# A fused decoder layer on one core: attention values multiplied for two pairs of heads at a time, with a new order of the small steps around them

## What is computed

```python
x = x + attn(layernorm(x))        # h = rmsnorm(.); q, k, v = h @ wq, wk, wv (16 heads of 64)
                                  # softmax(q k^T / 8) v, then w_out, b_out
x = x + xattn(k=v=ctx, q=layernorm(x))   # one head of 128 over 512 rows, then Wo, bo
x = x + ffn(layernorm(x))         # quant_linear -> relu -> quant_linear
# quant_linear: x to 0..255 by the maximum of the WHOLE x, w to int8 by the row's maximum
```

## Time and profile before

| | us |
|---|---|
| median of 3 runs (402.93 to 403.12) | 403.11 |
| the profiled execution | 403.67 |
| its span on the core | 401.7 |
| TensorE busy | 379.6 (94%) |
| VectorE busy | 325.9 (81%) |
| ScalarE busy | 259.6 (65%) |
| GpSimd busy | 164.0 (41%) |

### The profile page before, as it was taken

How to read it: one execution, slowest core, us unless ns; L and a number is a source line. 1 busy time by engine, 2 the same in 40 slices (tenths; PEclk the granted TensorE clock), 3 DMA queues, 4 the chain that set the end, 5 groups by cost and what they waited for, 6 DMA issues and landing times.

```text
span 401.7 us, 9053 instructions
## 1 busy us (share of the span) xinstructions
PE 379.6 (94%) x2983; PEld 286.1 (71%) x2983; DVE 325.9 (81%) x777; ACT 259.6 (65%) x807; POOL 164.0 (41%) x179
## 2 busy tenths in 40 slices
PE   8899999999999999999999999999999999988675
PEld 7678777787777777777778777777777767656222
DVE  4869778869897789869895989778986998557895
ACT  4967676756768556767675666756676776515574
POOL 3645534534544345434454444434542444401000
PEclk9989999999999999999999999999999999999699
DMA  7500000001000100001000100010000000000003
GB/s 234 147 15 2 2 2 0 2 3 39 2 3 0 41 0 0 0 0 39 0 0 0 39 0 0 0 39 0 0 0 0 28 1 2 0 2 0 0 2 104
DMA packets 12310, 7.50 MB, mean 19 GB/s; under 512 B 1280, under 2 KB 11264, under 8 KB 12288
## 3 DMA queue, kind: packets, MB, share of 16 engines
q1 hardware_dynamic: 11856, 6.69, 5.6%
q10 hardware_dynamic: 432, 0.52, 0.5%
HBM read 6.16 MB, written 1.05 MB: 18 GB/s over the span
## 4 chain that ended last, share of the span: by engine, by line
PE 64%; DVE 20%; issue 10%; ACT 4%; DVEq 1%; POOL 1%; POOLq 0%; ACTq 0%
PE turned_bank L460 13%; PE o_bank L469 12%; PE score L450 11%; PE acc_bank L476 5%; DVE pT L911 4%; DVE negmax L904 4%; PE side_bank L433 3%; PE q_bank L433 3%; PE side_bank L527 3%; PE q_bank L435 3%; PE q_bank L434 3%; DVE h_max L1220 2%; PE side_bank L434 2%; PE side_bank L435 2%; PE side_bank L523 2%
## 5 line engine op out<-in xcount | busy, mean ns | idle before, releaser
L1264 POOL TENSOR_TENSOR prob<-prob,rinv 128x512 f32<-128x512 f32 x128 | 132.6, 1043 | 149.5 <-DVE rinv L908 149.4
L725 ACT ACTIVATE prob<-score,negmax 128x256 f32<-128x256 f32 x252 | 117.3, 473 | 71.8 <-DVE negmax L904 70.1
L904 DVE TENSOR_REDUCE negmax<-score 128x2 f32<-128x512 f32 x126 | 85.8, 682 | 28.1 <-PE score L450 26.8
L911 DVE COPY pT<-turned_bank 128x512 f32<-128x512 f32 x128 | 86.9, 679 | 11.5 <-PE turned_bank L460 11.1
L460 PE MATMUL turned_bank<-ident,prob 128*128 128x128 f32 x512 | 84.1, 287 | 3.9 <-DVE pT L911 3.4
L460 PEld LDWEIGHTS turned_bank<-ident,prob 128*128 128x128 f32 x512 | 53.9, 141 | 37.4 <-issue 26.0
L469 PE MATMUL o_bank<-pT,v_sb 128*64 128x256 f32 x512 | 69.4, 392 | 0.8 <-DVE pT L911 0.8
L725 ACT ACTIVATION_READ_ACCUMULATOR prob<-score,negmax 128x1 f32 x252 | 50.9, 202 | 0.0
L716 ACT ACTIVATE q_hi<-q_bank 128x512 fp32r<-128x512 f32 x63 | 38.0, 603 | 11.9 <-PE q_bank L435 11.0
L469 PEld LDWEIGHTS o_bank<-pT,v_sb 128*64 128x64 f32 x512 | 31.0, 136 | 19.9 <-issue 7.2
L896 DVE TENSOR_TENSOR q_lo<-q_bank,q_hi 128x512 fp32r<-128x512 f32 x63 | 42.7, 680 | 0.0
(11 more groups left out here) (229 smaller groups left out, 614.8 us busy)
## 6 DMA issues: line engine op xcount, KB each, us to landing
c_sb<-in_ctx_dram SPq DMA_DIRECT2D x8, 256.0 KB, 3.0
x_sb<-in_x_dram SPq DMA_DIRECT2D x8, 128.0 KB, 2.7
out_dram<-xn_all SPq DMA_DIRECT2D x4, 256.0 KB, 2.3
big<-in_L_attn_wk_dram ACTq DMA_DIRECT2D x2, 256.0 KB, 4.7
big<-in_L_attn_wq_dram SPq DMA_DIRECT2D x2, 256.0 KB, 5.7
big<-in_L_attn_wv_dram SPq DMA_DIRECT2D x2, 256.0 KB, 6.4
wo_sb<-in_L_attn_w_out_dram SPq DMA_DIRECT2D x1, 512.0 KB, 7.7
w_sb<-in_L_ffn_w_dram SPq DMA_DIRECT2D x2, 256.0 KB, 4.7
```

The lines of the kernel that those rows point to most:

```text
L725: last = nc.scalar.activation(prob[:, slot, t, :], banks[r][:, t * S:(t + 1) * S], ACT.Exp, bias=negmax[:, slot, t:t + 1], scale=1.0, accu ...
L904: nc.vector.tensor_reduce(negmax[:, slot], banks[r][:].rearrange("p (t k) -> p t k", k=S), X_AXIS, ALU.max, negate=True).then_inc(max_done, 1)
L911: nc.vector.tensor_copy(pT[:, slot].rearrange("p k q -> p (k q)"), turned_bank[:]).then_inc(pT_done, 1)
L1264: nc.gpsimd.tensor_tensor(prob[:, slot], prob[:, slot], rinv[:, slot].unsqueeze(2).to_broadcast([P, QT, S]), ALU.mult).then_inc(prob_done, 1)
```

## The change

In even steps TensorE now multiplies the values of two pairs, into both halves of `o_bank`, and ScalarE copies both with one instruction; in odd steps TensorE takes the output projections of two pairs. `pT` has 8 places in place of 4 for this. ScalarE does an even step's second side task after both exponentials, where it stood between them. VectorE does `split_lo` ahead of the maxima, where it stood behind them; in step 1 the `residual` stands behind the maxima, and `aggregate(1)` and GpSimd's `inverse_root(1)` move from step 1 to step 2. At the start `weights_lo(0, 1, 4)` comes before the third inversion. In the last batch the last three steps turn through three banks, `TL` moves from (7,0) to (7,1), rounding the feed-forward weights moves from step 3 to behind the steps, and the last two values use a bank each. In the feed-forward block two `keep_warm` are added, and both products of the second half have a bank for each chunk.

```diff
-LAST_PLACE[7, 0] = "TL"
+LAST_PLACE[7, 1] = "TL"
-        pT = sb("pT", [P, 4, QT, S])
+        pT = sb("pT", [P, 8, QT, S])
-        yT_banks = [q_banks[0], o_bank]
-        y_banks = [side_bank, score_bank[0]]
+        yT_banks = [q_banks[0], o_bank, *pT_bank]
+        y_banks = [side_bank, *score_bank, acc_bank]
+        def turned_in(kind, j, r):
+            if late(kind, j):          # kind == "last" and j >= PAIRS - 3
+                return (turned_bank, *q_banks)[(2 * (j - PAIRS + 3) + r) % 3]
+            return turned_bank
+        def copied_before(kind, g, j, r):
+            return 2 * g + r - (2 if late(kind, j) and (j > PAIRS - 3 or r) else 0)
# TensorE, step
-                if cross and j == 1:
-                    pe.wait_ge(o_done, g - 1)
-                    project_out(PAIRS - 1)
...
-                wait(pe, pT_done, 2 * g)
-                turn_probs(2 * j % 8)
+                wait(pe, pT_done, copied_before(kind, g, j, 0))
+                turn_probs(2 * j % 8, turned_in(kind, j, 0))
+                no_scores = kind == "last" and j >= PAIRS - 2
+                if no_scores:
...
+                    turn_probs(2 * j % 8 + 1, turned_in(kind, j, 1))
+                halves = b * (PAIRS // 2) + j // 2
+                if j % 2 == 0 and not (kind == "first" and j == 0):
+                    wait(pe, o_done, halves - 1)
...
+                    for n in range(2):
+                        last = values((j - 2 + n) % PAIRS, 1 - parity if j == 0 else parity, o_bank[:, n * S:(n + 1) * S])
+                    last.then_inc(o_raw, 1)
+                if j % 2 == 1 and not (kind == "first" and j == 1):
+                    pe.wait_ge(o_done, halves)
...
+                    project_out((j - 3) % PAIRS)
                     project_out((j - 2) % PAIRS)
                 if task := side_at(kind, j, 1):
                     side(kind, b, 1 - parity, i, task)
-                    values((j - 1) % PAIRS, (slot, slot + 1), 1 - parity if j == 0 else parity)
# TensorE, behind the steps
+            values(PAIRS - 2, LAST % 2, o_bank[:, 0:S]).then_inc(o_raw, 1)
             pe.wait_ge(pT_done, B * H)
+            values(PAIRS - 1, LAST % 2, score_bank[0][:, 0:S]).then_inc(o_raw, 1)
...
             turn_rows(pT_bank[1], NT - 4, QT)
+            keep_warm(10, ident[:], ident[:], side_bank[:, 0:P])
             spread_max(0, acc_bank[:, P:2 * P])
             pe.wait_ge(xn3_done, B)
             turn_rows(pT_bank[0], NT - 2, QT)
+            keep_warm(4, ident[:], ident[:], side_bank[:, 0:P])
...
-                if n >= 1:
-                    turn_back(n - 1)
-            turn_back(CHUNKS - 1)
+            for n in range(CHUNKS):
+                turn_back(n)
# ScalarE, step
-                if task := side_at(kind, j, 1):
+                if j % 2 == 1 and (task := side_at(kind, j, 1)):
                     side(kind, b, 1 - parity, task)
                 if more_scores:
                     act.wait_ge(max_done, 2 * g + 6)
                     exps(1, (2 * j + 5) % 8)
+                if j % 2 == 0 and (task := side_at(kind, j, 1)):
+                    side(kind, b, 1 - parity, task)
+                if j % 2 == 0 and not (kind == "first" and j == 0):
+                    act.wait_ge(o_raw, b * (PAIRS // 2) + j // 2)
+                    copy(oT[:].rearrange("p n q -> p (n q)"), o_bank[:]).then_inc(o_done, 1)
# VectorE, step
                 if cross and j == 2:
+                    aggregate(1, b, *PLAIN_NORM)
+                if ahead(kind, j, 3) and not (kind == "first" and j == 0):
+                    dve.wait_ge(q_hi_done, g + 4)
+                    split_lo((j + 3) % 2, q_banks[(j + 3) % 2])
+                if cross and j == 2:
                     normalise(1, tiles(xn2), tiles(x1_sb), b, xn2_done)
...
-                if cross and j == 1:
-                    residual(b, 1 - parity)
                 if more_scores:
                     dve.wait_ge(score_raw, 2 * g + 5)
                     maxima(0, (2 * j + 4) % 8)
...
                 if cross and j == 1:
-                    aggregate(1, b, *PLAIN_NORM)
-                if ahead(kind, j, 3):
-                    dve.wait_ge(q_hi_done, g + 4)
-                    split_lo((j + 3) % 2, q_banks[(j + 3) % 2])
+                    residual(b, 1 - parity)
# VectorE, start and behind the steps
+            weights_lo(0, 1, 4)
             dve.wait_ge(exp_done, 3)
             invert_sums(2)
-            weights_lo(0, 1, 4)
             over_batches(dve, step)
+            round_weights()
# GpSimd, step
-                if cross and j == 1:
+                if cross and j == 2:
                     inverse_root(1, b)
```

More of the change, by code:

```diff
@@ L700, in _ @@
             for n in range(CHUNKS):
-                wait(pe, yT_done, n - 1)
                 for c in range(FT):
@@ L1035, in step @@
                 more_scores = ahead(kind, j, 2)
-                if ahead(kind, j, 1):
+                if ahead(kind, j, 1) and not (kind == "first" and j == 0):
                     dve.wait_ge(exp_done, 2 * g + 4)
@@ L1056, in step @@
                 dve.wait_ge(pT_raw, 2 * g + 1)
-                keep_turned(2 * j % 4)
+                keep_turned(2 * (j % 4), turned_in(kind, j, 0))
+                if kind == "first" and j == 0:
+                    dve.wait_ge(exp_done, 4)
+                    invert_sums(3)
+                no_scores = kind == "last" and j >= PAIRS - 2
+                if no_scores:
+                    dve.wait_ge(pT_raw, 2 * g + 2)
+                    keep_turned(2 * (j % 4) + 1, turned_in(kind, j, 1))
                 if more_scores:
@@ L1083, in step @@
                     cross_norm(b)
-                if kind == "last":
-                    weights(j)
+                if kind == "last" and j == 0:
+                    weight_scales()
             dve.wait_ge(load_x[0], 16)
```

107 lines of the change are left out of this document (53 added, 54 removed).

## The result

The changed kernel takes 425.89 us in the median (425.37 to 426.36, 4 runs), beside 403.12 us (402.93 to 403.13) of the kernel before on the same chip: 1.057 times as long, 95% interval 1.055 to 1.058. The forecast was 418.7, in a range of 401 to 424: the sign and the places are right, the size is too small by a third, and the time lies above the range.

A forecast was written before the change was run, and what follows sets the result against it. TensorE was taken to set the loop's pace, with VectorE having little to spare. Loop 18.0, start -2.0, first batch +0.5, last batch 0, then -0.5 and -0.4 gave +15.6 us: 419.3, less 0.56, so 418.7 us; range 401 to 424.

The forecast's parts named there:

- What TensorE saves: Loop: pairing saves one entry into and one exit from values per two steps, 0.65 us a batch, bounds 0 and 1.0.
- Sum of the waits: Loop batch: five TensorE waits, 0.95 + 0.8 + 0.65 + 1.1 + 0.85 = 4.35 us, less 0.4 already there.
- the loop term: Six loop batches: 3.3 us each, taken as 3.0 with a shade off for overlaps; +18.0, bounds -6 and +24.
- Step 7's: Step 7, turn 1: OX starts later behind two groups of values, VectorE's maximum is 0.9 late, turn 1 waits 0.95 us.
- W1's and QX's: Steps 1 and 3: ScalarE's high halves come behind head 1's exponentials, so W1 waits 0.8 us and QX 1.1.
- Start -2.0: First step: weights_lo ahead of an inversion brings turn 1's copy 0.8 us earlier; -2.0 us, bounds 0 and -2.5.
- First batch +0.5: First batch, no cross attention: step 3 waits 0.9 us, three odd steps 0.1 each, less 0.65; +0.5 us.
- Last batch 0: Last batch: steps 0 to 4 lose +2.3 us, waits behind step 5 go for -2.5; taken as 0, bounds -2.5 and +2.
- The sum's -0.5: The -0.5 us in the forecast's sum, standing ahead of the -0.4 taken for the last addition and stores.
- (b): Rival: TensorE stays the bound and the new order is hidden; faster, about -8 us, 395 us; chance 0.17.
- (c): Rival: only step 7's and step 3's QX wait stay; +6 us in the loop, -2.4 elsewhere, 406.7 us; chance 0.15.
- (d): Rival: worse, the walk leaves out waits of next scores or pairing saves nothing; +24 or more, 426 us; chance 0.10.

The follow-up runs named there:

- moves, no pairing: Kernel before with the changed kernel's ends and its moves on VectorE, ScalarE and GpSimd, but one pair's values and one projection per step: 431.44 us.
- pairing, OX first: Kernel before with pairing and the changed kernel's ends, without the low-half, root and ScalarE moves; side task OX ahead of step 6's values: 408.14 us.
- the same, norms on ScalarE: Kernel with pairing, ends and OX ahead of the values, with normalise of both norms made by ScalarE instead of VectorE: 399.70 us.
- ends, norms on ScalarE: Also called the control: kernel before with only the changes at both ends, both norms' normalise on ScalarE, no pairing: 395.74 us.
- the kernel with the ends: Kernel before with only the changes at both ends (start, last batch, feed-forward block), none of those in the loop: 398.66 us.

## Why the prediction fell short

By starts of each step's first projection (step 1 from W1, step 0 to W1), one loop batch of the same kind, in us:

| kernel | 1 | 2 | 3 | 4 | 5 | 6 | 7 | 0 | all |
|---|---|---|---|---|---|---|---|---|---|
| before | 4.38 | 5.24 | 5.09 | 5.61 | 5.40 | 6.43 | 4.95 | 6.49 | 43.59 |
| changed | 3.71 | 6.25 | 6.93 | 5.98 | 4.66 | 6.89 | 5.57 | 7.55 | 47.54 |
| moves, no pairing | 4.25 | 6.35 | 6.94 | 5.98 | 5.81 | 6.43 | 5.13 | 7.54 | 48.43 |
| pairing, OX first | 3.72 | 6.64 | 5.08 | 6.23 | 4.66 | 6.85 | 4.53 | 7.04 | 44.75 |
| the same, norms on ScalarE | 3.72 | 5.94 | 4.73 | 6.24 | 4.67 | 6.85 | 4.53 | 7.02 | 43.70 |
| ends, norms on ScalarE | 4.38 | 5.16 | 4.83 | 5.39 | 5.38 | 6.43 | 4.96 | 6.52 | 43.05 |

**What TensorE saves.** Right in kind, too small. Steps 5 and 6 of the changed kernel wait for nothing and take 11.55 for 11.83 us, 0.28 less; times four that is 1.1 a batch, estimated, where 0.65 was taken (its upper end was 1.0).

**The waits.** This step failed: "Sum of the waits: 4.35 ... less what was there (0.4)", and the shade off it. The idle rows of two batches sum to 4.64 a batch (1.13 + 0.88 + 0.48 + 0.95 + 0.42 + 0.78); TH's 0.42 is missing in my walk. I took 0.4 for what was there, it shows 0.19. And I priced a wait at its idle time. With 1.1 saved, a batch that is 3.95 longer must hold 5.0 of delay more than before, 0.6 more than the idle rows: delays like those that TH's row and the control made visible. Six rows of waits that are each short by 0.1 to 0.2 are enough for that (an estimate from the delays measured above). So the loop term is 3.95 a batch against 3.0, 23.6 against +18.0, and the shade went the wrong way. This is 5.6 of the 7.2 us by which the time was missed. That 23.6 is nearly the term's upper bound, +24, is luck: the bound stood for a pairing that saves nothing.

**Where each wait comes from.** Step 7's by way of OX, `veps` and the low half: right (1.13 for 0.95), and each link alone carries some of it: OX 0.43, the low half 0.59, `veps` 1.0 by the starts. W1's and QX's by way of ScalarE's order: right (0.88 and 0.95 for 0.8 and 1.1). Step 2's for GpSimd's root: only 0.2 of the 0.48 (0.65 forecast). Step 3's turn 1: 0.78 for 0.85, of which the low half carries 0.35. The cover of an odd step is about as I drew it, since in the kernel with the moves and no pairing no turn 1 shows idle time (by the starts, that of step 7 is 0.2 late); but I held the thin cover for the cause. Without it the loss is larger, because the side tasks then meet the late halves and the late `normalise`. The 2.6 that I gave an even step leaves out its side task: turn 0 to turn 1 is 3.01 in step 6 (234.00 to 237.01). The walk also counts 1.0 a batch as won by moving `normalise` away from GpSimd's scalings, 1.62 less 0.60. Of this step 2's row gives all (0.60 for 1.62, behind 1.06 of idle time for the root), but step 3's takes 0.4 of it back (1.72 for 1.31).

**Start, first and last batch.** Start -2.0: right, -2.2 in the kernel with the ends. First batch +0.5: wrong, +2.55. Last batch 0: -1.6, and -3.0 in the kernel with the ends alone. The two errors nearly cancel, which is luck.

**Feed-forward block and end.** The sum's -0.5, which rivals (b) and (c) hold too, was an estimate for ten products in the gap that raise the granted clock. No run shows it by itself: the products stand in every kernel with the ends, beside the other changes there. With them the spread maximum takes 0.49 us behind 0.47 idle us, where it took 0.80 behind 2.70, and two neighbouring products of the feed-forward block start 0.22 apart where it was 0.42, at a granted clock of 1.00 for 0.50. That is 0.3 less on the one and 0.2 on the distance of the others, the size of the term. The two products, before and changed:

```profile
377.21 0.63 PE L681 MATMUL turned_bank<-xrT,w_qT 128*128 128x512 f16 x1
377.63 0.63 PE L681 MATMUL q_bank<-xrT,w_qT 128*128 128x512 f16 x1
```

```profile
398.93 0.39 PE L703 MATMUL turned_bank<-xrT,w_qT 128*128 128x512 f16 x1
399.15 0.39 PE L703 MATMUL q_bank<-xrT,w_qT 128*128 128x512 f16 x1
```

But the stores crowd by 1.0 where 0.4 net was to be won: -0.3 for -0.9 together.

**Rivals.** (b) is refuted in the loop: every wait of the forecast was there. (d) said that the walk leaves waits out, and its 426 is the time measured, though the waits left out were other ones (TH's, and what no row shows); 0.10 was too little, and the range should have gone beyond it, since all that I had left out was on that side.

**Open.** Why the pairing still loses 4 us to the control with both norms on ScalarE (steps 2, 3 and 4 are longer than the control's by 0.78, -0.10 and 0.85, where the pairing by itself would give +0.42, -0.7 and +0.42) was not taken further; its turns of steps 2 and 3 wait 0.32 and 0.37. Its trace shows one more place: turn 1 of step 7 starts 1.17 behind the two projections, where the side task of step 5 follows them after 0.89, and no row shows it as idle. So step 7 is 0.42 us shorter than the control's, where the thinner odd step 5 is 0.71.

## What to carry to other kernels

An engine that is busy 43.1 of 43.6 us is not for that reason its own bound: moving a neighbour's stretched rows away made a batch of the same products 0.5 us shorter. Before work is taken in larger groups on the full engine, list for each result how long it may be late, and price a missed one by the distance of starts, not by the idle time shown. Moves that are made to fit a new order are worth a run without it: here they cost more than the order, and the two cheap ends and two rows given to ScalarE were the gain.

## What the runs showed that was not expected

- `veps`, 128x2, took 0.97 us on VectorE beside GpSimd's scaling, 0.17 to 0.27 in steps 0 and 2, and 0.20 on ScalarE; the low half, 128x512 with one input from a bank, 0.66 beside the same scaling. The width of a row says little of its price there.
- Idle time shown ahead of a product is short of the delay by starts by 0.1 to 0.2 us (0.95 for 1.07, 0.34 for 0.51), and smaller delays show nothing.
- Three moves that each cost 10.6 to 14.7 us by themselves cost 32.8 together, nearly their sum of 36.1, in a kernel where TensorE had looked like the only bound.
